# A two-layer graph network on 64 graphs: the last pair in halves, the last seven steps in an order of their own

## The reference, cut to what matters

```python
h = relu(layernorm(x))
# layer 0: graph attention with 4 heads, then one output head
h = elu(gat(h, adj, W_heads, a_heads))      # 4 heads of 256, joined to 1024
out = elu(gat(h, adj, W_out, a_out))        # 1024 -> 256
ffn = relu(out @ w1 + b1) @ w2 + b2
x = x + layernorm(ffn + out) * gamma + beta
# layer 1: a linear graph layer
h = relu(layernorm(x))
mi, mj = h @ Wi.T, h @ Wj.T
x = x + deg * (mi + b) + adj @ mj
# gat: Wh = h @ W; e = leaky(f1[i] + f2[j]), masked by adj; softmax(e) @ Wh
```

## Time and profile before

| | us |
|---|---|
| median of 3 runs | 872.32 |
| profiled execution, its time | 870.21 |
| its span, first to last instruction | 868.3 |
| PE busy | 849.3 |
| DVE busy | 701.7 |
| POOL busy | 693.6 |
| ACT busy | 668.0 |

### The profile page before, as it was taken

The page is one execution under the profiler, slowest core; times in us unless marked ns, Lnnn a source line. Parts: engine busy times, 40 slices in busy tenths (PEclk is TensorE's granted clock), DMA queues, the critical chain, the costliest instruction groups (busy, mean ns, idle before and its releaser), DMA issues.

```text
span 868.3 us, 20346 instructions
## 1 busy us (share of the span) xinstructions
PE 849.3 (98%) x6400; PEld 785.6 (90%) x6400; DVE 701.7 (81%) x2002; ACT 668.0 (77%) x1801; POOL 693.6 (80%) x944
## 2 busy tenths in 40 slices
PE   8799999999999999999999999999999999999986
PEld 5599999999999999999999999999999999999963
DVE  5877888888888888888888888888888888877764
ACT  4789878878887887888788788778878877776642
POOL 2579888888888888888888888888888888888862
PEclk7899999999999999999999999999999999999999
DMA  6200010111110011111001111100111110000000
GB/s 197 74 13 26 26 36 3 39 37 39 37 38 27 13 37 39 38 38 38 25 15 37 37 39 37 39 20 19 37 37 37 38 38 17 10 26 26 25 25 24
DMA packets 29976, 30.46 MB, mean 35 GB/s; under 512 B 1808, under 2 KB 29472, under 8 KB 29872
## 3 DMA queue, kind: packets, MB, share of 16 engines
q1 hardware_dynamic: 29808, 29.11, 11.0%
q0 software_dynamic: 64, 0.07, 0.0%
HBM read 20.78 MB, written 8.39 MB: 34 GB/s over the span
## 4 chain that ended last, share of the span: by engine, by line
PE 94%; POOL 2%; DVE 1%; ACT 1%; issue 1%; POOLq 0%; ACTq 0%; DVEq 0%
PE ps L1222 84%; PE ps L1340 4%; PE ps L1414 2%; PE ps L1296 2%; PE ps L1395 2%; PE ps L1362 1%; PE ps L1210 1%; ACT lend L968 0%; ACT lend L957 0%; PE ps L1181 0%; DVE res L510 0%; POOL wo L425 0%; POOL lend L409 0%; POOL h_lo L375 0%; DVE lend L734 0%
## 5 line engine op out<-in xcount | busy, mean ns | idle before, releaser
L375 POOL TENSOR_TENSOR h_lo<-h2v,h_hi 128x512 fp32r<-128x512 f32 x128 | 165.1, 1291 | 49.9 <-ACT h_hi L992 49.8
L1222 PE MATMUL ps<-gh_hi,wh_hi 128*128 128x256 f32 x512 | 152.5, 298 | 1.6 <-DVE gh_lo L601 1.6
L1222 PE MATMUL ps<-wo_hi,h_hi 128*128 128x258 f32 x512 | 150.3, 294 | 0.0
L1222 PE MATMUL ps<-wo_lo,h_hi 128*128 128x258 f32 x512 | 144.4, 282 | 0.0
L1222 PE MATMUL ps<-gh_hi,wh_lo 128*128 128x256 f32 x512 | 144.3, 282 | 0.0
L1222 PE MATMUL ps<-wo_hi,h_lo 128*128 128x258 f32 x512 | 144.1, 281 | 0.0
L1222 PE MATMUL ps<-gh_lo,wh_hi 128*128 128x256 f32 x512 | 143.6, 280 | 0.0
L601 DVE TENSOR_TENSOR gh_lo<-ps,gh_hi 128x512 fp32r<-128x512 f32 x128 | 88.4, 691 | 52.4 <-ACT gh_hi L935 52.2
L646 DVE SCALAR_TENSOR_TENSOR h2v<-h2e,ps 128x512 f32<-128x512 f32 x128 | 87.7, 685 | 16.9 <-POOL h2e L381 16.8
L957 ACT ACTIVATE lend<-lend,zm 128x128 f32<-128x128 f32 x256 | 98.9, 391 | 3.0 <-DVE zm L663 3.0
L1222 PEld LDWEIGHTS ps<-wo_lo,h_hi 128*128 128x128 f32 x512 | 97.3, 190 | 4.4
(11 more groups left out here) (171 smaller groups left out, 2725.6 us busy)
## 6 DMA issues: line engine op xcount, KB each, us to landing
xa<-in_x SPq DMA_DIRECT2D x32, 256.0 KB, 3.7
xr<-in_x SPq DMA_DIRECT2D x32, 256.0 KB, 2.9
out<-res SPq DMA_DIRECT2D x32, 256.0 KB, 3.2
lend<-in_L_gnn_W_heads SPq DMA_DIRECT2D x4, 256.0 KB, 4.5
wo<-in_L_gnn_W_out SPq DMA_DIRECT2D x1, 1024.0 KB, 8.0
l1w_sb<-in_L_gnn_W SPq DMA_DIRECT2D x1, 512.0 KB, 8.0
lend<-in_L_gnn_w SPq DMA_DIRECT2D x2, 256.0 KB, 3.6
oe<-in_L_gnn_a_out SPq DMA_DIRECT2D x1, 256.0 KB, 8.9
```

The lines of the kernel that those rows point to most:

```text
L375: pool.tensor_tensor(h2_lo[:, u, :, :].rearrange("p c n -> p (c n)"), h2v[u % 2][:, :], h2_hi[:, u, :, :].rearrange("p c n -> p (c n)").bi ...
L1222: return pe.matmul(out_, lhs, rhs, start=start, stop=stop)
```

## The change

Steps 0 to 31 are written out as before. The last seven steps are no longer made by `one`: each engine has a function `last()` that lists its remaining work call by call, in an order of its own. The calls are those of before, except for pair 31 behind W_out, which is done in halves:

- `out2`, `out_exp`, `out_less`, `out_elu`, `ov_high` by halves of the output features, each half in a PSUM bank of its own. The subtraction for `ov_lo` is on DVE instead of POOL (`ov_low_here`).
- `hidden_by_rows` and `ffn_by_rows` do the products by halves of the summed dimension, as these become ready; `hidden_relu`, `hidden_whole` and the subtraction (`hidden_low_here`, DVE instead of POOL) go by halves.
- the normalisation of norm 2 and norm 3 is on DVE (`normal_here`, one tensor_scalar per graph) instead of ACT, and waits for the reciprocal deviation only, not for the shift. `scale2`, `residual2` and the statistics go by graph. The relu of norm 3 moves into `h3t_high` and `h3t_low`.
- `h3_transposes`, `h3t_high`, `h3t_low`, the product (`mixed_high` for what needs h3_hi only, `mixed_low` for the rest), `gather_half`, `result` and `store_half` go by graph, with banks of their own.

First halves have semaphores of their own. `gather` of pair 28 moves behind the last `wh2_part` of pair 31. 22 fillers stand in the tail instead of 41. Cut to its core:

```diff
+LAST_STORES = 2
+HEAD, TAIL = 0, 32
...
+B_OUT_LAST, B_HIDDEN_LAST = (B_OUT, 1), (B_HIDDEN, 2)
+B_H3T_LAST, B_LAST_LAST = (B_H3T, 1), (B_LAST, 2)
...
+        first_half = {n: sem(n + "_first_half") for n in (
+            "out_done out_exp out_less out_elu ov_hi ov_lo hidden_lo "
+            "normal2_scaled x2_ready h3t_done h3t_hi h3t_lo last_done result_ready").split()}
...
+        def wait_part(eng, name, p, s):
+
+            if s is None:
+                wait(eng, name, p)
+            elif name in first_half:
+                if s == 0:
+                    eng.wait_ge(first_half[name], 1)
+                else:
+                    wait(eng, name, p)
+            else:
+                wait(eng, name, p, s + 1)
...
+        def halves(s, bank, banks):
+
+            if s is None:
+                return ps[:, bank, :].rearrange("p (c n) -> p c n", c=2)
+            return ps[:, banks[s], s * F:(s + 1) * F].unsqueeze(1)
...
 
-            for t in range(PAIRS + STAGES - 1):
+            for t in range(HEAD, TAIL):
...
+            def last():
+                load_residual(pair(29)); store(pair(25)); load_residual(pair(30)); store(pair(26)); load_residual(pair(31)); store(pair(27))
+                store(pair(28)); store(pair(29)); store(pair(30)); store_half(pair(31), 0); store_half(pair(31), 1)
+
             steps(one)
-            for e in range(2):
-                sp.wait_ge(stored[e], PAIRS // 2 * 16)
+            last()
+            sp.wait_ge(stored[0], PAIRS // 2 * 16)
+            sp.wait_ge(stored[1], (PAIRS // 2 + LAST_STORES - 1) * 16)
...
+            def out_less(p, s=None):
+
+                wait_part(pool, "out_exp", p, s)
+                pool.tensor_scalar(oe[:, part(s), :], oe[:, part(s), :], 1.0, -1.0, ALU.mult, ALU.add).then_inc(part_done("out_less", s), 1)
...
+                ov_low(pair(29)); elu_less(pair(31), 0); elu_less(pair(31), 1); rstd3(pair(28)); hidden_low(pair(29)); h2_low(pair(31), 0)
+                elu_less(pair(31), 2); h2_low(pair(31), 1); elu_less(pair(31), 3); rstd2(pair(29)); h2_low(pair(31), 2); h2_low(pair(31), 3)
+                out_less(pair(30)); scale2(pair(29)); ov_low(pair(30)); rstd3(pair(29)); add_beta(pair(30)); hidden_low(pair(30)); add_bias(pair(29))
+                rstd2(pair(30)); out_less(pair(31), 0); out_less(pair(31), 1); scale2(pair(30)); rstd3(pair(30)); add_bias(pair(30))
+                add_beta(pair(31)); rstd2(pair(31)); scale2(pair(31), 0); scale2(pair(31), 1); rstd3(pair(31)); add_bias(pair(31))
+
             steps(one)
...
+            def ov_low_here(p, s):
+
+                wait_part(dve, "ov_hi", p, s)
+                dve.tensor_tensor(ov_lo[:, part(s), :], ov[:, part(s), :], ov_hi[:, part(s), :].bitcast(F32), ALU.subtract)\
+                   .then_inc(part_done("ov_lo", s), 1)
...
+            def normal_here(name, p, dst, src, mv, rs, done, s):
+
+                wait(dve, name + "_rstd", p)
+                dve.tensor_scalar(dst[p.e][:, s, :], src, mv[p.e][:, s, 0:1], rs[p.e][:, s:s + 1], ALU.subtract, ALU.mult).then_inc(S[done], 1)
+
+            def norm2_here(p, s):
+
+                wait(dve, "x2_ready", p, lag=1)
+                normal_here("ffn", p, lt, y[:, s, :], b_mv, b_rs, "normal2_ready", s)
...
+                wait_part(dve, "h3t_hi", p, s)
+                n = nodes(s)
+                t = ps[:, B_H3T if s is None else B_H3T_LAST[s], :].rearrange("p (c n) -> p c n", c=C)[:, :, n]
+                if s is None:
+                    dve.tensor_tensor(h3_lo[:, :, n], t, h3_hi[:, :, n].bitcast(F32), ALU.subtract).then_inc(S["h3t_lo"], 1)
+                else:
+                    dve.scalar_tensor_tensor(h3_lo[:, :, n], t, 0.0, h3_hi[:, :, n].bitcast(F32), ALU.max, ALU.subtract)\
+                       .then_inc(part_done("h3t_lo", s), 1)
...
+                norm2_var(pair(30)); add_mi(pair(29), 0); out_elu(pair(31), 0); mj_low(pair(29), 0); out_elu(pair(31), 1); mj_low(pair(29), 1)
+                add_mi(pair(29), 1); ov_low_here(pair(31), 0); residual2(pair(30)); ov_low_here(pair(31), 1); norm3_stats(pair(30))
+                norm3_var(pair(30)); hidden_whole(pair(31), 0); hidden_whole(pair(31), 1); hidden_low_here(pair(31), 0); result(pair(29))
+                hidden_low_here(pair(31), 1); h3t_low(pair(30)); add_b2(pair(31)); norm2_stats(pair(31)); norm2_var(pair(31)); add_mi(pair(30), 0)
+                mj_low(pair(30), 0); norm2_here(pair(31), 0); norm2_here(pair(31), 1); mj_low(pair(30), 1); residual2(pair(31), 0)
+                residual2(pair(31), 1); norm3_stats(pair(31), 0); norm3_stats(pair(31), 1); norm3_var(pair(31)); add_mi(pair(30), 1); result(pair(30))
+                norm3_here(pair(31), 0); norm3_here(pair(31), 1); h3t_low(pair(31), 0); h3t_low(pair(31), 1); add_mi(pair(31), 0); mj_low(pair(31), 0)
+                mj_low(pair(31), 1); add_mi(pair(31), 1); result(pair(31), 0); result(pair(31), 1)
...
+                act.activation(h3_hi[:, :, n], ps[:, B_H3T if s is None else B_H3T_LAST[s], :].rearrange("p (c n) -> p c n", c=C)[:, :, n],
+                               ACT.Copy if s is None else ACT.Relu)\
+                   .then_inc(part_done("h3t_hi", s), 1)
...
+                norm3(pair(28)); elu_exp(pair(31), 2); score_leaky2(pair(30)); h3t_high(pair(28)); soft_exp2(pair(30)); h2_high(pair(31), 1)
+                h2_high(pair(31), 2); elu_exp(pair(31), 3); mj_high(pair(28), 0); a2_copy(pair(30)); h2_high(pair(31), 3); norm2(pair(29))
+                mj_high(pair(28), 1); out_exp(pair(30)); ov_high(pair(30)); wh2_copy(pair(31), 0); wh2_copy(pair(31), 1); hidden_relu(pair(30))
+                norm3(pair(29)); score_leaky2(pair(31)); h3t_high(pair(29)); soft_exp2(pair(31)); a2_copy(pair(31)); mj_high(pair(29), 0)
+                out_exp(pair(31), 0); out_exp(pair(31), 1); norm2(pair(30)); mj_high(pair(29), 1); ov_high(pair(31), 0); ov_high(pair(31), 1)
+                hidden_relu(pair(31), 0); hidden_relu(pair(31), 1); norm3(pair(30)); h3t_high(pair(30)); mj_high(pair(30), 0); mj_high(pair(30), 1)
+                h3t_high(pair(31), 0); h3t_high(pair(31), 1); mj_high(pair(31), 0); mj_high(pair(31), 1)
...
+            def hidden_by_rows(p, c):
+
+                wait_part(pe, "ov_lo", p, c)
+                if c == 0:
+                    wait_bank(p, ("scores_masked", 2, -3), ("mi_added", 2, 2))
+                for dc in range(C):
+                    cols = slice(dc * P, (dc + 1) * P)
+                    last = three(ps[:, B_HIDDEN_LAST[dc], dc * 2 * P:(dc + 1) * 2 * P], (w1_hi[:, c, cols], w1_lo[:, c, cols]),
+                                 (ov_hi[:, c, :], ov_lo[:, c, :]), c == 0, c == C - 1)
+                    if c == C - 1:
+                        last.then_inc(S["hidden_done"], 1)
+
...
+            def ffn_by_rows(p, c):
+
+                wait_part(pe, "hidden_lo", p, c)
+                for b in range(2):
+                    rows = slice(b * P, (b + 1) * P)
+                    last = three(ps[:, B_FFN, b * F:(b + 1) * F], (hid_hi[:, c, rows], hid_lo[:, c, rows]),
+                                 (w2_hi[:, c, :], w2_lo[:, c, :]), False, b == 1 and c == C - 1)
+                if c == C - 1:
+                    last.then_inc(S["ffn_done"], 1)
...
+            def mixed_high(p, b):
+
+                wait_part(pe, "h3t_hi", p, b)
+                if b == 0:
+                    wait_bank(p, ("at_lo", 1, -4), ("ht_copied", 1, -5), ("mj_lo", 1, 1))
+                if b == 1:
+                    wait_bank(p, ("scores_masked", 1, -5), ("hidden_full", 2, -1), ("mi_added", 2, 1))
+                rows = slice(b * P, (b + 1) * P)
+                for c in range(C):
+                    for k, w in enumerate((l1w_hi, l1w_lo)):
+                        mm(ps[:, B_M[b], :].rearrange("p (s o) -> p s o", s=2), h3_hi[:, c, rows], w[:, :, c, :], c == k == 0, False)
+
+            def mixed_low(p, b):
+
+                wait_part(pe, "h3t_lo", p, b)
+                rows = slice(b * P, (b + 1) * P)
+                for c in range(C):
+                    last = mm(ps[:, B_M[b], :].rearrange("p (s o) -> p s o", s=2), h3_lo[:, c, rows], l1w_hi[:, :, c, :], False, c == C - 1)
+                last.then_inc(S["m_done"], 1)
+
+            def gather_half(p, s):
+
+                wait_part(pe, "mj_lo", p, s)
+                wait_bank(p, ("at_lo", 2, -4), ("probs2_copied", 1, -2), ("h3t_lo", 1, 0))
+                mm(ps[:, B_LAST_LAST[s], s * F:(s + 1) * F], adj_t[:, :], mj_hi[:, s, :], True, False)
+                mm(ps[:, B_LAST_LAST[s], s * F:(s + 1) * F], adj_t[:, :], mj_lo[:, s, :], False, True).then_inc(part_done("last_done", s), 1)
...
+                h2_unit(pair(31), 0, 0); h2_unit(pair(31), 0, 1); h2_unit(pair(31), 1, 0); h2_unit(pair(31), 1, 1); score_rows2(pair(30))
+                hidden(pair(29), 0); hidden(pair(29), 1); ffn_out(pair(29)); scores2(pair(30)); h2_unit(pair(31), 2, 0); h2_unit(pair(31), 2, 1)
```

(12 more changed lines are left out.)

270 lines of the change are left out of this document (178 added, 92 removed).

## The result

The changed kernel takes 866.48 us, the median of 17 runs, against 871.03 in 17 runs of the kernel before beside them: a ratio of 0.9944 with a 95% interval from 0.9930 to 0.9958, so 3.7 to 6.1 us. The ratio leaves out one of the 17 executions, which took 4252.07 us for a reason that no trace shows. The forecast was 868.3, a gain of 4.0 us on a median of 872.32 from three runs. Of the 1.8 us between forecast and result 1.3 lie in that starting median. The profiled execution has a span of 862.4 us and a time of 864.18.

The account below looks back on a forecast made before the run. Bound: a full PE queue up to the last W_out matmul, then 41.7 us behind it, ending in pair 31's chain. Gains of 4.3 less 0.3 for waits gave 4.0 us, from 872.32 to 868.3; range 866.9 to 869.6, chance 0.68.

Parts of the forecast that it names:

- more than forecast: Rival: halves on POOL and DVE interleave, small scalar operations run faster, queue waits are shorter; 1.5 us more, 866.8; chance 0.07.
- Waits in the full stretch: Steps 32 to 35, PE without idle time: waits made by the new order cost 0.3 us, bounds 0 and 1.5.
- The three places that I called tight: Full stretch: mixed(27,0) after h3t_low, prob_transposes2(29) after out2(29), h2_unit(29,0,0) after gh_unit(29,3); each nominally met or missed by 0.1 us.
- W_out to the transposes of pair 31: Behind W_out: gather(28)'s 0.47 us is lost again, prob_transposes2(31) starts at 833.87 instead of 834.50; gain 0.6 us.
- the queue walk: Method for new times: walking the new queues with traced durations and a hand-off of 0.03 to 0.05 us from end to start.
- Out2 to hidden: Pair 31 in halves, held by POOL and ACT queues: hidden starts 840.15 instead of 841.40, its last matmul gains 0.8 us.
- Norm 2: Pair 31 after ffn, norm on DVE, scale2 and residual2 in halves: 2.9 us from the root; summed as 0.8 us gain.
- Norm 3 to mixed: Pair 31, moments of x2 to the end of mixed: 5.7 us instead of 7.78, gain 2.05, the largest single term.
- Result and store: Pair 31's end: mj to result 2.16 us against 2.38, gain 0.2; half-size last store 0.2, bounds no gain and 0.4.
- Fillers at nothing: Tail filler matmuls, 41 before and 22 after, cost nothing because the chain's own wait covers them; uncovered, about 0.23 us each.
- the clock: Rival: PE's matmul clock halves in the tail from about 838, 875.3 us; slower if before about 845; chance 0.04.
- The rivals of waits and of no effect: Late tight hand-offs in the full stretch, 870.7, chance 0.16; chain hanging on pairs 29 and 30, 872, chance 0.05.

Follow-up runs that it names:

- the order alone: New order of the last seven steps with pair 31's steps whole on their old engines, against the kernel before: 872.91 us, ratio 1.0019.
- the norms elsewhere: Changed kernel with pair 31's norms 2 and 3 back on ScalarE, fillers as they were: tail 134.92 us against 132.35.
- the three kernels that had lost the clock: New order with pair 31 whole, halves in the old order, changed kernel with norms on ScalarE: tails 139.28, 139.34, 134.92; with more fillers 137.55, 136.45, 133.51.

## Why the prediction was right, step by step

The direction and the size of the gain came as forecast, somewhat larger. The time of 866.48 us lies 0.4 below the range that I gave the forecast (866.9 to 869.6), next to the 866.8 of "more than forecast". With 871.03 in place of 872.32 as the start the same sum gives 867.0 and a range of 865.6 to 868.3, which holds it.

*Waits in the full stretch: wrong, and small.* I took 0.3 us; PE has none. The three places that I called tight were met. The gather moved behind W_out gave 0.40 of 0.47.

*W_out to the transposes of pair 31: 0.58 us gained behind W_out, forecast 0.16.* The step that failed is the queue walk: I let each instruction start at the shown end of the one before it. VectorE's timeline of the changed kernel:

```profile
824.79 0.42 DVE L873 TENSOR_TENSOR mj_lo<-ps,mj_hi 128x256 fp32r<-128x256 f32 x1
825.13 0.48 DVE L880 SCALAR_TENSOR_TENSOR lend<-ps,deg,lend 128x256 f32<-128x256 f32 x1
825.52 0.74 DVE L655 BATCH_NORM_STATS2 c_st<-lend 128x6 f32<-128x256 f32 x2
826.18 0.37 DVE L663 BATCH_NORM_AGGREGATE c_mv<-c_st 128x2 f32<-128x6 f32 x2
826.49 0.69 DVE L890 TENSOR_TENSOR res<-lend,ps 128x512 f32<-128x512 f32 x1
827.10 0.15 DVE L676 COPY g_cols<-ps 128x4 f32<-128x4 f32 x1
```

Each starts 0.06 to 0.09 us before the last has ended. Counted from the common point, result(28) came at 96.44 us, forecast 96.69, and wh2_scores(31) at 97.05, forecast 97.39: 0.25 and 0.34 of the 0.42 us by which the stretch was mis-sized.

*Out2 to hidden: 0.97 gained, forecast 0.62; hidden to the end of ffn 0.54, forecast 0.36.* The mechanism held (halves, with POOL and ACT queues ahead of them), the sizes were short by about 0.5 us together. GpSimd came to out_less(31) at 105.92 instead of 106.44, since all that leads to it was earlier. That the overlap of neighbouring instructions is the whole reason was not tested. A reading was off too: the last hidden matmul before ends at 843.08 (842.80 and 0.28), not 842.9. ffn's end to the moments lost 0.52, forecast 0.64: add_b2(31) does stand behind h3t_low(30).

*Norm 2: 0.91 gained up to residual2, forecast 0.87.* From the root on I had 2.9 us, it took 2.76. For a tensor_scalar the row of 0.35 in the earlier trace rows was nearer than the doubled rate that the Trainium skill gives (VectorE: DVE Perf Modes, "The perf-mode tier table"): two norms take 0.73 back to back, a single one 0.40, and no doubled rate shows. The two halves of scale2 took 1.52 (forecast 1.54). The halves of residual2 took 1.27 together, the faster one 0.41: the first began beside scale2's second and ended behind it.

*Norm 3 to mixed: 1.65 gained, forecast 2.05.* The largest term, and mis-sized: 6.13 us, not 5.7. The transposes start 1.64 us behind the moments instead of 1.5 (the norm's first half takes 0.41, not 0.35), and from there to the end it is 4.49 instead of 4.21: behind the wait for its copy the first 512-column product stands 0.33 ahead of the next (854.54 and 854.87), and so in the second half, where I had taken 0.235 for each. Whole, the stretch is 1.9 us longer, so the forecast's source is shown.

*Result and store: 0.46 and 0.22, forecast 0.2 and 0.2.* I had both halves of result behind the last gather. The first one needs only the first gather and stands behind add_mi(31,1): it starts at 859.29, beside the last gather's second matmul (859.26 to 859.54).

*Fillers at nothing: wrong as a rule, right in this kernel.* My reason was that the chain's own wait covers them, and so that taking some out costs nothing either. What 22 fillers hold up is worth 2.4 us of tail. That taking 19 of 41 out was free fits the shorter waits that the halves leave (the order alone, with the same seven ahead of the transposes, lost the clock); fewer or more of them in the changed kernel itself were not tried, except for none. I gave the clock 0.04 as a rival. It did not come, but its mechanism stood next to the changed kernel: 2.95 us of bare wait with the norms elsewhere lost the clock. My argument against it was that the longest wait is shorter than one that the clock survived (2.26 us). That does not hold: 1.80 us kept it in the changed kernel, and 1.79 us lost it without fillers. That the clock stayed is then in part luck. The point of return that I gave (before 845 us, for a slower kernel) was not tried; with fillers back, the tails of the three kernels that had lost the clock were 1.4 to 2.9 us shorter.

The rivals of waits and of no effect fell. "More than forecast" is what the tail shows: 1.3 us more than the 4.0 of the sum. Of the reasons that I gave it the shorter waits for result(28) and rstd2(30) are seen; the small scalar operations were no faster (the root took 1.08 us, forecast 1.07), and residual2's first half did end behind scale2's second. How much of the 1.3 the overlap of neighbouring instructions makes up was not measured.

## What to carry to other kernels

In the tail of a pipeline, what a part is worth depends on what stands ahead of it in the queues: here order and halves gave 0.1 to 0.6 and 1.2 us alone and 5.3 together. Whoever tries parts one by one must set the fillers anew for each and look at the granted clock, or the matmul clock decides the comparison. And in walking a queue, take the distance from start to start of neighbouring instructions, not their durations.
